# Loads of x in odd tiles dealt unevenly over the DMA engines, in a field-pair projection kernel

## Chip, core and metric

The kernel runs on one core of a Trainium2 chip. The metric is the device time of one execution in microseconds; for a program on one core that is the time of that core. The core has 16 DMA engines, numbered 0 to 15 in this text, and all its queues (SyncE's, ScalarE's, GpSimd's) send their work to these 16.

## What is computed

```python
# r_x: 2048 x 32 x 64 float32; W: 496 x 64 x 64 float32
PAIRS = list(combinations(range(32), 2))      # 496 pairs (i, j), i < j
xi = x[:, pi, :]                              # 2048 x 496 x 64
xj = x[:, pj, :]
proj = jnp.einsum('bpd,pod->bpo', xi, W)
return proj * xj                              # 2048 x 496 x 64
```

For each of 496 pairs of fields, field i is projected by the pair's 64x64 matrix and multiplied, element by element, by field j. The result has 2048 rows of 496 x 64 float32, 260 MB, and is by far the largest thing that moves; x is 16.8 MB and the weights 8.1 MB.

## The kernel before

The batch is cut into 16 tiles of 128 rows, and a row of the batch is a partition of SBUF. The weights are loaded once, in 13 pieces, into `w_sb`. A tile needs its x twice: as it is (`x_sb0` for even tiles, `x_sb1` for odd ones, 128 rows of 8 KB each), and turned (`x_t`), so that TensorE can multiply by it.

A tile is 21 steps (`plan`), each of which fills two halves of a PSUM buffer (`proj`, 2 buffers x 2 halves). TensorE (`project`) writes both halves. VectorE multiplies the first half by x and writes the product to a staging buffer (`staged`, L338). The second half goes the same way in every third step and in the last; in the other 14 (`pool_steps`) ScalarE copies it to the staging buffer (L258) and GpSimd multiplies it there by x (L232). Between step 9 and step 10 stands the item "turn": TensorE transposes the next tile's x (L270), and ScalarE copies the result to `x_t` (L247).

The steps are put together in 11 groups, and each group ends in one store of 128 rows (SyncE, L191), of 896 to 1952 KB; 11 stores a tile, 176 in all. The staging has 9 slots: groups 9 and 10 use the slots of groups 4 and 5. Before a slot is written again, `slot_free` waits until the store that reads it has landed on all engines (semaphore `stored`, 16 counts per store).

Each engine has its own instruction stream in program order, and each DMA issuer too. x is loaded as follows. The first tile's x comes in two halves from SyncE at the start (L195, L197). The second tile's x is the last DMA of SyncE's prologue (L205), 1 MB with 128 rows of 8 KB. From tile 1 on, GpSimd issues the load of the next tile's x (`load_x`, L219) ahead of its work of step 3 (`LOAD_BEFORE`), once VectorE and GpSimd have finished the tile before: 128 rows in one DMA, 14 times, for tiles 2 to 15. In an odd tile the next x goes to `x_sb0`, in an even one to `x_sb1`. TensorE waits for it ahead of the turn (L304, semaphores `x_loaded0` and `x_loaded1`). ScalarE issues one DMA in all, the identity for the transposes (L242).

The lines that the change touches are these; SyncE's last prologue load and GpSimd's load:

```python
sp.dma_start(x_sb[1][:], x[P:2 * P, :]).then_inc(x_second_loaded, 16)
...
pool.wait_ge(emptied[b][1], use + 1)
pool.wait_ge(pool_scaled[group_of[pool_steps[-1]]], tile.number)
pool.dma_start(x_sb[1 - tile.parity][:], x[bass.ds((tile.number + 1) * P, P), :]
              ).then_inc(x_loaded[1 - tile.parity], 16)
```

Of the kernel before, what the change touches and what calls it, by code (L numbers as in the profile page):

```python
# [9 lines left out]
P = 128  # L10
# [3 lines left out]
LOAD_BEFORE = 3  # L14
WARM_UP = 16

SHARED_SLOTS = {9: 4, 10: 5}


def pair_index(i, j, fields):  # L20
# [51 lines left out]
def field_pair_project(nc, x, w, ident, out, fields, dim):  # L72
    batch = x.shape[0]
    tiles = batch // P
# [11 lines left out]
    def items(tile):  # L86


        for n, item in enumerate(last_tile if tile.last else whole_tile):
            yield item, (1 + n) % 2, tile.number * per_tile + (1 + n) // 2  # L90


    pool_steps = [s for s in range(len(steps) - 1) if s % 3 != 2]
    group_of = {s: g for g, group in enumerate(groups) for s in group}

    def group_range(g):
        segments = [seg for s in groups[g] for unit in steps[s] for seg in unit]
        first = min(pair_index(i, j, fields) for i, j, _ in segments)
        assert sum(n for _, _, n in segments) == max(
            pair_index(i, j, fields) + n for i, j, n in segments) - first  # L100
        return first, sum(n for _, _, n in segments)

    slot_of = [SHARED_SLOTS.get(g, g) for g in range(len(groups))]
    slots = len(groups) - len(SHARED_SLOTS)
    assert sorted(set(slot_of)) == list(range(slots))
# [13 lines left out]
    def every_tile(emit):  # L119

        for t in range(tiles):
            emit(Tile(t, t % 2, t // 2, last=t == tiles - 1))

    def each_tile(eng, emit):

        emit(Tile(0, 0, 0))
        with eng.Fori(0, (tiles - 2) // 2) as t:
            emit(Tile(2 * t + 1, 1, t))
            emit(Tile(2 * t + 2, 0, t + 1))
        emit(Tile(tiles - 1, 1, tiles // 2 - 1, last=True))  # L130

    with ExitStack() as ctx:  # L132
        def sb(name, shape, dt=F32):
            return ctx.enter_context(nc.sbuf_tensor(name, shape, dt))

        def sem(name):
            return ctx.enter_context(nc.semaphore(name))
# [3 lines left out]
        x_sb = [sb(f"x_sb{h}", [P, fields * dim]) for h in range(2)]  # L141
# [7 lines left out]

        ident_loaded = sem("ident_loaded")  # L150
        x_first_loaded = [sem(f"x_first_loaded{h}") for h in range(2)]
        x_second_loaded = sem("x_second_loaded")

        x_loaded = [sem(f"x_loaded{h}") for h in range(2)]
        w_loaded = [sem(f"w_loaded{c}") for c in range(len(w_cuts) - 1)]
        filled = [[sem(f"filled{b}{h}") for h in range(2)] for b in range(2)]
        emptied = [[sem(f"emptied{b}{h}") for h in range(2)] for b in range(2)]

        pool_scaled = [sem(f"pool_scaled{g}") for g in range(len(groups))]
# [11 lines left out]
        def staged_part(s, i, j, n):  # L171
            g = group_of[s]
            to = (pair_index(i, j, fields) - group_range(g)[0]) * dim
            return staged[slot_of[g]][:, to:to + n * dim]

        @block.sync
        def _(sp):
            def emit(tile):
                where = {item: (b, use) for item, b, use in items(tile)}
                for g, group in enumerate(groups):  # L180
                    first, n = group_range(g)


                    pooled = any(s in pool_steps for s in group)
                    if pooled and g == 0:
                        sp.wait_ge(pool_scaled[g], tile.number + 1)
                    b, use = where[group[-1]]
                    sp.wait_ge(emptied[b][group[-1] not in pool_steps], use + 1)
                    if pooled and g > 0:
                        sp.wait_ge(pool_scaled[g], tile.number + 1)  # L190
                    sp.dma_start(out[bass.ds(tile.number * P, P), first * dim:(first + n) * dim],  # L191
                                 staged[slot_of[g]][:, 0:n * dim]).then_inc(stored[slot_of[g]], 16)

            half = fields * dim // 2
            sp.dma_start(x_sb[0][:, 0:half], x[0:P, 0:half]).then_inc(x_first_loaded[0], 16)  # L195
            sp.dma_start(w_sb[:, w_cuts[0]:w_cuts[1]], w[:, w_cuts[0]:w_cuts[1]]).then_inc(w_loaded[0], 16)
            sp.dma_start(x_sb[0][:, half:], x[0:P, half:]).then_inc(x_first_loaded[1], 16)  # L197
            for c in range(1, len(w_cuts) - 2):
                sp.dma_start(w_sb[:, w_cuts[c]:w_cuts[c + 1]], w[:, w_cuts[c]:w_cuts[c + 1]]
                             ).then_inc(w_loaded[c], 16)  # L200

            c = len(w_cuts) - 2
            sp.dma_start(w_sb[0:dim, w_cuts[c]:w_cuts[c + 1]], w[0:dim, w_cuts[c]:w_cuts[c + 1]]
                         ).then_inc(w_loaded[c], 16)
            sp.dma_start(x_sb[1][:], x[P:2 * P, :]).then_inc(x_second_loaded, 16)  # L205

            every_tile(emit)
            for k in range(slots):
                sp.wait_ge(stored[k], 16 * slot_uses[k] * tiles)

        @block.gpsimd
        def _(pool):
            def load_x(tile):

                _, b, use = list(items(Tile(tile.number - 1, 1 - tile.parity, None)))[-1]

                pool.wait_ge(emptied[b][1], use + 1)
                pool.wait_ge(pool_scaled[group_of[pool_steps[-1]]], tile.number)
                pool.dma_start(x_sb[1 - tile.parity][:], x[bass.ds((tile.number + 1) * P, P), :]  # L219
                              ).then_inc(x_loaded[1 - tile.parity], 16)  # L220

            def emit(tile):
                for item, b, use in items(tile):
                    if item == LOAD_BEFORE and not tile.first and not tile.last:
                        load_x(tile)
                    if item not in pool_steps:
                        continue
                    for i, j, n in steps[item][1]:
                        product = staged_part(item, i, j, n)

                        pool.wait_ge(emptied[b][1], use + 1)
                        last = nc.gpsimd.tensor_tensor(  # L232
                            product, product, x_sb[tile.parity][:, j * dim:(j + n) * dim], ALU.mult)
                    g = group_of[item]
                    if item == max(s for s in groups[g] if s in pool_steps):
                        last.then_inc(pool_scaled[g], 1)

            every_tile(emit)

        @block.scalar  # L240
        def _(act):
            act.dma_start(ident_sb[:], ident).then_inc(ident_loaded, 16)  # L242

            def turned_out(b, use, to):
                for h in range(2):
                    act.wait_ge(filled[b][h], use + 1)
                    nc.scalar.activation(x_t[to][:, h * (UNIT // P):(h + 1) * (UNIT // P), :].rearrange(  # L247
                        "p k b -> p (k b)"), proj[b][h][:], ACT.Copy).then_inc(emptied[b][h], 1)

            def emit(tile):  # L250
                for item, b, use in items(tile):
                    if item == "turn":
                        turned_out(b, use, 1 - tile.parity)
                    elif item in pool_steps:
                        (i, j, n), = steps[item][1]
                        slot_free(act, tile, group_of[item])
                        act.wait_ge(filled[b][1], use + 1)  # L257
                        nc.scalar.activation(staged_part(item, i, j, n), proj[b][1][:, 0:n * dim],  # L258
                                             ACT.Copy).then_inc(emptied[b][1], 1)

            turned_out(0, 0, 0)
            every_tile(emit)

        @block.tensor
        def _(pe):
# [31 lines left out]
            def emit(tile):  # L297
                for item, b, use in items(tile):
                    if item == "turn":

                        if tile.first:
                            pe.wait_ge(x_second_loaded, 16)
                        else:
                            pe.wait_ge(x_loaded[1 - tile.parity], 16 * (tile.half + tile.parity))  # L304
                        for h in range(2):
                            pe.wait_ge(emptied[b][h], use)
                            turn(b, 1 - tile.parity, h)
                    else:
                        project(tile, item, b, use)
# [64 lines left out]
```

## Time and profile before

| what | value |
|---|---|
| time, median of 3 runs | 690.63 us (690.4 to 691.05) |
| the profiled execution's own time | 690.38 us |
| its span, first to last instruction | 688.5 us |
| around the span | 1.9 us |
| TensorE busy | 591.9 us (86%) |
| VectorE, GpSimd, ScalarE busy | 412.2, 398.4, 207.4 us |
| DMA, mean over the span | 285.24 MB, 414 GB/s |
| stores and other traffic of SyncE's queue (q1) | 270.28 MB, 94.1% of 16 engines' span |
| GpSimd's queue (q0) | 14.68 MB, 5.1% |
| mean granted TensorE clock | 0.922 |

The share of DMA is the mean busy share of the 16 engines. A transfer's time is counted from its packet's start to its end, so that an engine that takes packets of two queues in turn counts a little twice; a share of 1.01 means that no engine stood idle. One engine of 16 alone is a share of 0.0625.

### The profile page before, as it was taken

What the parts mean: (1) busy time and instruction counts of PE and PEld (TensorE: products, weight loads), DVE (VectorE), ACT (ScalarE), POOL (GpSimd) and SP (SyncE); (2) the same over time, 40 slices, a digit from 0 to 9 for tenths busy, and PEclk for the clock granted to TensorE, in tenths of its full rate; (3) what the DMA queues carried; (4) which work ended last, traced back from release to release, by engine and by line L of the source; (5) the groups of instructions that cost most, each with busy time, mean ns of one, the idle gap of its engine ahead of it and who ended that gap; (6) DMA issues with size and microseconds to landing.
All of it is one profiled execution on the core that took longest, in us unless ns stands there. A gap on an engine that the chain in (4) does not pass through costs nothing.

```text
span 688.5 us, 7590 instructions
## 1 busy us (share of the span) xinstructions
PE 591.9 (86%) x2704; PEld 365.3 (53%) x2704; DVE 412.2 (60%) x528; ACT 207.4 (30%) x257; POOL 398.4 (58%) x242
## 2 busy tenths in 40 slices
PE   6969897988979799797997979899797997989962
PEld 4536464545555465465555545465464655555531
DVE  1646574774738657374684747657475683747751
ACT  2412333233222333233233232332332333232320
POOL 0745575574655846476574655846466574755841
PEclk9998999999989989898999999999898998989985
DMA  8999999999999999999999999999999999999995
GB/s 341 391 428 428 420 427 421 427 419 427 428 416 429 415 426 421 422 427 420 428 416 429 424 415 428 399 426 385 410 429 413 428 420 428 430 412 428 421 425 244
DMA packets 29765, 285.24 MB, mean 414 GB/s; under 512 B 3312, under 2 KB 3440, under 8 KB 7216
## 3 DMA queue, kind: packets, MB, share of 16 engines
q1 hardware_dynamic: 27584, 270.28, 94.1%
q0 software_dynamic: 2016, 14.68, 5.1%
q14 instruction: 16, 0.13, 0.0%
q8 instruction: 5, 0.08, 0.0%
q10 hardware_dynamic: 144, 0.07, 0.0%
HBM read 24.97 MB, written 260.05 MB: 414 GB/s over the span
## 4 chain that ended last, share of the span: by engine, by line
PE 46%; DMA 38%; POOL 7%; ACT 4%; DVE 3%; issue 1%; DVEq 0%; ACTq 0%; SPq 0%
PE proj L292 42%; DMA out_dram<-staged 26%; DMA x_sb<-x_dram 11%; POOL staged L232 7%; ACT staged L258 3%; PE proj L270 3%; DVE staged L338 3%; DMA ident_sb<-ident_dram 1%; PE proj L313 1%; ACT x_t L247 0%; ACTq L257 0%; DVEq L132 0%; DVEq L335 0%; SPq L190 0%
## 5 line engine op out<-in xcount | busy, mean ns | idle before, releaser
L338 DVE TENSOR_TENSOR staged<-proj,x_sb 128x1024 f32<-128x1024 f32 (+7 forms) x528 | 412.2, 828 | 265.5 <-PE proj L292 220.3
L292 PE MATMUL proj<-w_sb,x_t 64*128 64x512 f32 (+7 forms) x2432 | 537.4, 543 | 26.3 <-DVE staged L338 24.8
L232 POOL TENSOR_TENSOR staged<-staged,x_sb 128x1024 f32<-128x1024 f32 (+4 forms) x224 | 390.6, 1753 | 275.0 <-ACT staged L258 272.5
L292 PEld LDWEIGHTS proj<-w_sb,x_t 64*128 64x128 f32 x2432 | 315.7, 193 | 242.9 <-issue 134.5
L258 ACT ACTIVATE staged<-proj 128x1024 f32<-128x1024 f32 (+4 forms) x224 | 173.7, 787 | 382.3 <-PE proj L292 329.7
L270 PE MATMUL proj<-ident_sb,x_sb 128*128 128x128 f32 x256 | 52.1, 388 | 52.2 <-DMA x_sb<-x_dram 52.2
L270 PEld LDWEIGHTS proj<-ident_sb,x_sb 128*128 128x128 f32 x256 | 46.4, 205 | 61.4 <-DMA x_sb<-x_dram 61.4
L247 ACT ACTIVATE x_t<-proj 128x1024 f32<-128x1024 f32 x32 | 32.4, 1023 | 80.5 <-PE proj L270 80.5
L313 PE MATMUL proj<-ident_sb 128*128 128x128 f32 x16 | 3.7, 425 | 5.7 <-DMA ident_sb<-ident_dram 5.7
L219 POOL DMA_DIRECT2D x_sb<-x_dram x14 | 8.4, 601 | 0.0
L313 PEld LDWEIGHTS proj<-ident_sb 128*128 128x128 f32 x16 | 3.3, 228 | 5.6 <-DMA ident_sb<-ident_dram 5.6
L247 ACT ACT_TABLE_LOAD x1 | 1.3, 1283 | 1.2 <-PEq L368 1.2
L368 POOL MEMSET const-float32-0.0<- 128x1 f32 x1 | 0.1, 98 | 0.2 <-issue 0.2
L368 POOL MEMSET const-bfloat16-1.0<- 128x1 bf16 x1 | 0.1, 101 | 0.0
L368 POOL MEMSET const-uint8-127<- 128x1 uint8 x1 | 0.1, 101 | 0.0
L368 POOL MEMSET const-float32-1.0<- 128x1 f32 x1 | 0.1, 98 | 0.0
## 6 DMA issues: line engine op xcount, KB each, us to landing
out_dram<-staged SPq DMA_DIRECT2D x16, 1952.0 KB, 14.4
out_dram<-staged SPq DMA_DIRECT2D x16, 1824.0 KB, 16.4
out_dram<-staged SPq DMA_DIRECT2D x16, 1728.0 KB, 13.6
out_dram<-staged SPq DMA_DIRECT2D x16, 1696.0 KB, 17.0
out_dram<-staged SPq DMA_DIRECT2D x16, 1568.0 KB, 16.5
out_dram<-staged SPq DMA_DIRECT2D x16, 1440.0 KB, 17.8
out_dram<-staged SPq DMA_DIRECT2D x16, 1312.0 KB, 11.8
out_dram<-staged SPq DMA_DIRECT2D x16, 1216.0 KB, 12.4
```

The costliest lines, as they stand in the source:

```text
L219: pool.dma_start(x_sb[1 - tile.parity][:], x[bass.ds((tile.number + 1) * P, P), :]).then_inc(x_loaded[1 - tile.parity], 16)
L232: last = nc.gpsimd.tensor_tensor(product, product, x_sb[tile.parity][:, j * dim:(j + n) * dim], ALU.mult)
L247: nc.scalar.activation(x_t[to][:, h * (UNIT // P):(h + 1) * (UNIT // P), :].rearrange("p k b -> p (k b)"), proj[b][h][:], ACT.Copy).then_i ...
L258: nc.scalar.activation(staged_part(item, i, j, n), proj[b][1][:, 0:n * dim], ACT.Copy).then_inc(emptied[b][1], 1)
L270: last = nc.tensor.transpose(proj[b][h][:, n * P:(n + 1) * P], x_sb[of][:, k * P:(k + 1) * P], ident_sb[:])
L292: last = nc.tensor.matmul(proj[b][h][:, at:at + width], x_t[tile.parity][half, i // 2, :], w_sb[half, col:col + width], start=True, stop=True)
L313: nc.tensor.transpose(proj[1][0][:, 0:P], ident_sb[:], ident_sb[:])
L338: last = nc.vector.tensor_tensor(staged_part(item, i, j, n), proj[b][h][:, at:at + n * dim], x_sb[tile.parity][:, j * dim:(j + n) * dim], ...
L368: nc = bacc.Bacc("TRN2", target_bir_lowering=False, num_devices=1)
```

## The change

In odd tiles (1, 3, ... 13), the next x no longer comes in one DMA of 128 rows. GpSimd loads 120 rows, then 1 row; ScalarE loads the last 7 rows, ahead of its own work of step 3, after the same two waits as GpSimd's. In tile 13 the numbers are 105, 13 and 10. Even tiles load 128 rows in one DMA as before. The second tile's x in the prologue comes in three parts: 112 rows and 12 rows from SyncE, and 4 rows from GpSimd as its first DMA, ahead of all its work. Each of the parts has a wait of its own on TensorE ahead of the turn. By the names in the diff, GpSimd's 120 rows go to all engines but engine 3 (`LEFT_OUT`), and the one row behind them to engine 3.

```diff
+LEFT_OUT = 3
+IN_STEP = LEFT_OUT + 1
+X_ROWS = (120, 1, 7)
+X_LAST_ROWS = (105, 16 - LEFT_OUT, 7 + LEFT_OUT)
...
+    def x_rows(tile):
+
+        if not tile.parity:
+            return (P,), 0
+        of = X_LAST_ROWS if tile.number == tiles - 3 else X_ROWS
+        assert sum(of) == P
+        return of[:-1], of[-1]
...
-            sp.dma_start(x_sb[1][:], x[P:2 * P, :]).then_inc(x_second_loaded, 16)
+            for row, rows in ((0, P - 16), (P - 16, 16 - IN_STEP)):
+                sp.dma_start(x_sb[1][row:row + rows, :], x[P + row:P + row + rows, :]
+                             ).then_inc(x_second_loaded, 16)
...
-                pool.dma_start(x_sb[1 - tile.parity][:], x[bass.ds((tile.number + 1) * P, P), :]
-                              ).then_inc(x_loaded[1 - tile.parity], 16)
+                row = 0
+                for rows in x_rows(tile)[0]:
+                    pool.dma_start(x_sb[1 - tile.parity][row:row + rows, :],
+                                   x[bass.ds((tile.number + 1) * P + row, rows), :]
+                                   ).then_inc(x_loaded[1 - tile.parity], 16)
+                    row += rows
+
+            pool.dma_start(x_sb[1][P - IN_STEP:, :], x[2 * P - IN_STEP:2 * P, :]).then_inc(x_in_step, 16)
...
+            def load_x_rest(tile):
+
+                _, b, use = list(items(Tile(tile.number - 1, 1 - tile.parity, None)))[-1]
+
+                act.wait_ge(emptied[b][1], use + 1)
+                act.wait_ge(pool_scaled[group_of[pool_steps[-1]]], tile.number)
+                rows = x_rows(tile)[1]
+                act.dma_start(x_sb[1 - tile.parity][P - rows:, :],
+                              x[bass.ds((tile.number + 2) * P - rows, rows), :]).then_inc(x_rest_loaded, 16)
...
+                    if item == LOAD_BEFORE and not tile.first and not tile.last and x_rows(tile)[1]:
+                        load_x_rest(tile)
...
-                            pe.wait_ge(x_second_loaded, 16)
+                            pe.wait_ge(x_second_loaded, 32)
+                            pe.wait_ge(x_in_step, 16)
+                        elif tile.parity:
+                            pe.wait_ge(x_loaded[0], 32 * tile.half + 32)
+                            pe.wait_ge(x_rest_loaded, 16 * tile.half + 16)
                         else:
-                            pe.wait_ge(x_loaded[1 - tile.parity], 16 * (tile.half + tile.parity))
+                            pe.wait_ge(x_loaded[1], 16 * tile.half)
```

On GpSimd, tile 1, ahead of step 3. `TENSOR_TENSOR` is a product of L232 (before) or L259 (after), `x_sb<-x_dram` the load. Before:

```order
L232 TENSOR_TENSOR staged<-staged,x_sb 128x1024 [waits emptied11]
L232 TENSOR_TENSOR staged<-staged,x_sb 128x896 [waits emptied01]
L219 DMA x_sb<-x_dram 128x2048 [waits pool_scaled9,emptied01]
L232 TENSOR_TENSOR staged<-staged,x_sb 128x768 [waits emptied01]
L232 TENSOR_TENSOR staged<-staged,x_sb 128x1024 [waits emptied11] x2
```

On GpSimd, the same place, now:

```order
L259 TENSOR_TENSOR staged<-staged,x_sb 128x1024 [waits emptied11]
L259 TENSOR_TENSOR staged<-staged,x_sb 128x896 [waits emptied01]
L242 DMA x_sb<-x_dram 120x2048 [waits pool_scaled9,emptied01]
L242 DMA x_sb<-x_dram 1x16x128
L259 TENSOR_TENSOR staged<-staged,x_sb 128x768 [waits emptied01]
L259 TENSOR_TENSOR staged<-staged,x_sb 128x1024 [waits emptied11] x2
```

A second DMA stands behind the first, with no wait; it is one row, written in the instruction as 16 pieces of 128 elements (512 B). In tile 13 its place is taken by one of 13x2048, and the first one's by 105x2048.

On ScalarE, the same item of tile 1. `ACTIVATE staged<-proj` is the copy that GpSimd's products wait for. Before:

```order
L258 ACTIVATE staged<-proj 128x1024 [waits filled11,stored0]
L258 ACTIVATE staged<-proj 128x896 [waits filled01,stored0]
L258 ACTIVATE staged<-proj 128x768 [waits filled01,stored1]
L258 ACTIVATE staged<-proj 128x1024 [waits filled11,stored2]
```

On ScalarE, now:

```order
L297 ACTIVATE staged<-proj 128x1024 [waits filled11,stored0]
L297 ACTIVATE staged<-proj 128x896 [waits filled01,stored0]
L284 DMA x_sb<-x_dram 7x2048 [waits pool_scaled9,emptied01]
L297 ACTIVATE staged<-proj 128x768 [waits filled01,stored1]
L297 ACTIVATE staged<-proj 128x1024 [waits filled11,stored2]
```

A DMA that waits for GpSimd's and VectorE's last work of the tile before now stands between two copies, seven times in the program.

## Rows read from the trace of the kernel before

**Rows 1.** Busy time by stage; columns: each engine (instructions), TensorE's clock, DMA share, GB/s
```profile
core 0: us, PE busy (x) PEld busy (x) DVE busy (x) ACT busy (x) POOL busy (x), PEclk, DMA share, GB/s
...
200.00:430.00 230.00, 205.83 (x946) 126.78 (x945) 142.19 (x186) 72.23 (x90) 134.92 (x82) 0.93 1.01 423
...
480.00:670.00 190.00, 168.21 (x765) 102.84 (x761) 117.83 (x150) 58.06 (x73) 114.74 (x69) 0.92 1.01 422
```

**Rows 2.** The same view, the end of the program
```profile
680.00:681.00 1.00, 0.00 (x0) 0.00 (x0) 0.00 (x0) 0.00 (x0) 0.00 (x0) 0.50 0.85 350
681.00:682.00 1.00, 0.00 (x0) 0.00 (x0) 0.00 (x0) 0.00 (x0) 0.00 (x0) 0.50 0.13 56
682.00:683.00 1.00, 0.00 (x0) 0.00 (x0) 0.00 (x0) 0.00 (x0) 0.00 (x0) 0.50 0.06 27
...
686.00:687.00 1.00, 0.00 (x0) 0.00 (x0) 0.00 (x0) 0.00 (x0) 0.00 (x0) 0.50 0.07 29
687.00:688.00 1.00, 0.00 (x0) 0.00 (x0) 0.00 (x0) 0.00 (x0) 0.00 (x0) 0.50 0.02 7
```

**Rows 3.** The last store of the program: issue, and time to landing
```profile
L191 SPq DMA_DIRECT2D out_dram<-staged x1: 333/333/333, 677.7 to 677.7; - x1
...
DMA to landing us min/median/max: 10.2/10.2/10.2
```

**Rows 4.** DMA packets between 681 and 688.5 us
```profile
DMA packets 29, 0.20 MB, mean 26 GB/s; under 512 B 6, under 2 KB 6, under 8 KB 19
```

**Rows 5.** Busy time by stage again, the stretches with gaps in the DMA
```profile
433.00:435.00 2.00, 2.00 (x10) 1.04 (x7) 2.00 (x3) 0.72 (x1) 2.00 (x2) 1.00 0.93 389
474.00:476.00 2.00, 2.00 (x14) 1.15 (x11) 1.43 (x2) 0.59 (x1) 2.00 (x2) 1.00 0.97 410
476.00:478.00 2.00, 2.00 (x11) 1.15 (x8) 2.00 (x3) 0.81 (x1) 2.00 (x2) 1.00 0.45 189
478.00:480.00 2.00, 2.00 (x12) 1.27 (x11) 1.61 (x3) 0.48 (x1) 1.98 (x2) 1.00 0.96 379
```

**Rows 6.** The page's DMA queues: packets, MB, share of 16 engines' span
```profile
q14 instruction: 16, 0.13, 0.0%
q8 instruction: 5, 0.08, 0.0%
```

**Rows 7.** The chain that ended last, its end: start, duration, what
```profile
654.17 15.98 DMA out_dram<-staged
...
670.17 0.90 DVE staged L338
...
676.64 0.99 DVE staged L338 x3
```

**Rows 8.** DMA issues: GpSimd's loads of x (L219), then ScalarE's one DMA (L242)
```profile
L219 POOL DMA_DIRECT2D x_sb<-x_dram x14: 591/591/720, 65.4 to 600.1; - x14
...
DMA to landing us min/median/max: 11.8/13.3/13.6
```
```profile
L242 ACTq DMA_DIRECT2D ident_sb<-ident_dram x1: 406/406/406, 0.7 to 0.7; - x1
```

**Rows 9.** Who waited for whom over the span: total, times, longest
```profile
PE proj L270 <- DMA x_sb<-x_dram: 52.2, 15, 4.2
...
DVE staged L338 <- DMA out_dram<-staged: 41.3, 22, 7.1
```

**Rows 10.** Timeline, start of tile 13: ScalarE, GpSimd, VectorE
```profile
555.46 0.92 ACT L258 ACTIVATE staged<-proj 128x896 f32<-128x896 f32 x1 [1.12 <-PE proj L292]
558.47 0.81 ACT L258 ACTIVATE staged<-proj 128x768 f32<-128x768 f32 x1 [2.09 <-PE proj L292]
```
```profile
548.66 2.76 POOL L232 TENSOR_TENSOR staged<-staged,x_sb 128x640 f32<-128x640 f32 x2 [0.47 <-ACT staged L258]
...
559.37 1.82 POOL L232 TENSOR_TENSOR staged<-staged,x_sb 128x768 f32<-128x768 f32 x1
562.41 2.37 POOL L232 TENSOR_TENSOR staged<-staged,x_sb 128x1024 f32<-128x1024 f32 x1 [1.22 <-ACT staged L258]
```
```profile
551.13 4.61 DVE L338 TENSOR_TENSOR staged<-proj,x_sb 128x448 f32<-128x448 f32 x9 [1.61 <-DMA out_dram<-staged]
```

More of the change, by code:

```diff
@@ L152, in field_pair_project @@
         x_second_loaded = sem("x_second_loaded")
+        x_in_step = sem("x_in_step")
         x_loaded = [sem(f"x_loaded{h}") for h in range(2)]
+        x_rest_loaded = sem("x_rest_loaded")
         w_loaded = [sem(f"w_loaded{c}") for c in range(len(w_cuts) - 1)]
```

## The prediction

> **What bounds the kernel now.** First the busy times by stage [rows 1]. From 200 to 430 us and from 480 to 670 us the share of the 16 DMA engines is 1.01, at 423 and 422 GB/s, while no compute engine is full (TensorE, the fullest, 168.2 of 190 us). An engine's packets queue without a gap, so compute could be somewhat faster or slower and the time would not move: the sum of the DMA work sets it. TensorE's and VectorE's waits for DMA [rows 9] are the back-pressure of that, not a cause.
>
> Second, the end [rows 2], read second by second. Up to 681 us nearly all engines work (0.85). From 682 us to the end the share is 0.06 to 0.07, and one engine of 16 is 0.0625: one engine is still busy while 15 are done. The packets say the same: 29 in the last 7.5 us, at 26 GB/s [rows 4], which is 423/16. The last store is issued at 677.7 and lands 10.2 us later, at 687.9 [rows 3]. So one engine is late, and the program ends with it.
>
> How late? The shares from 680 us on are 0.85, 0.13, 0.06, five more of this size down to 0.02, together 1.32 engine-sets, or 21.1 engine-us. The late engine has 7.5 of these (to 687.4, and its completion comes at 687.9), which leaves 13.6 for 15 engines: on average they end at 680.9, the last of them at about 682 (the 0.13 of 681 to 682 is two engines). The late one ends 7.0 us behind their mean. Besides, the others ran dry twice before [rows 5]: at 433 to 435 us, 389 GB/s where 423 is full, is 0.16 us lost; at 474 to 480 us, 410, 189 and 379 make 0.06 + 1.11 + 0.21. Together 1.5 us for all 16, so 1.6 us for the 15. At such a point stores wait for slots, and a slot is free only when its store has landed on all engines. So the late engine's excess of work is 7.0 + 1.6 = **8.6 us** over the mean of the others.
>
> A part of it has a name: instruction fetches, 21 packets with 0.13 + 0.08 MB [rows 6], 7.9 us at 26.5 GB/s if one engine serves them all. That they sit on one engine is my reading; the trace does not number its engines.
>
> **The price of a row.** 8192 B at 423/16 = 26.4 GB/s is 0.31 us of one engine.
>
> **What moves.** With the dealing that the diff names, engine 3 has 2 rows of each odd tile's x in place of 8 (1 of GpSimd's, 1 of ScalarE's): 7 loads x 6 rows = 42 rows less. In the prologue, 112 rows give each engine 7, 12 rows give one more to engines 0 to 11, and 4 rows one more to 0 to 3, so engine 3 has 9 instead of 8. Net 41 rows, **12.7 us less** on engine 3. They go elsewhere: ScalarE's 7 rows put one more on engines 0, 1, 2, 4, 5 and 6, each time but with tile 13's own sums; with the prologue each of these six gets 7 rows more in all, **2.2 us**. Engines 7 to 9 get one row more, 10 and 11 none, 12 to 15 one less. The check: 6 x 7 + 3 - 4 - 41 = 0.
>
> That this is how rows are dealt no row of the trace before shows, since each DMA there has 128 rows (or 64). The Trainium skill ("DMA: Bandwidth & Descriptors", "Why a DMA increments its semaphore by 16 and not by 1") agrees for the large parts: the number of engines is the largest up to 16 that divides the rows, GpSimd's DMAs start where a round-robin cursor stands, ScalarE's and SyncE's at the lowest engine. By that, 4 rows bring the cursor to 4, and 120 rows take 15 engines from there, all but engine 3.
>
> **The sum.** If engine 3 is the late one, its 12.7 us relief is more than its excess of 8.6, so it ends before the others, and the bound is the fullest of the other 15. Their mean ends at 680.9, minus 1.6 for the dry stretches that the late engine caused, plus 2.2 for the six: 681.5. The last of the others ends some 1.1 us behind their mean (682.0 against 680.9); if it is one of the six, 682.6. I take 682.1, the middle. The last landing moves from 687.9 to 682.1, **5.8 us** less; the span goes to 682.7, the execution to 684.6 (690.38 - 5.8), and against the median of 690.63, 0.25 above the profiled run, it is 684.8. Bounds: 1.6 not won back gives 686.4; with engine ends levelled better (680.9 - 1.6 + 0.9, where 0.9 is the 42 rows shared by 15 engines) 683.0.
>
> **What is added, and its cover.** GpSimd gets a second DMA issue, 0.59 us [rows 8], in 7 tiles. Behind it stands the product of step 3; the next product then waited 1.22 us for ScalarE [rows 10], so the delay ends there. ScalarE gets a DMA issue (0.41 us, rows 8's other row) behind two waits. In tile 13 its copy ends at 556.4, GpSimd's last product of the tile before at 551.4 and VectorE's at 555.7, so both waits are over, and 2.09 us of idle time for TensorE follow [rows 10]: nothing queued behind it is late. The copies and GpSimd's products behind it are who would wait otherwise. If the cover were gone, these cost up to 7 x 1.0 = 7 us of compute, which a DMA share of 1.01 hides as long as the stores' queue holds work. SyncE's one more prologue issue (0.6 us) and GpSimd's 4 rows fall into the start, where SyncE issues nothing for 10 us afterwards; 4 rows ahead of the first loads cost at most 0.31 us on an engine. Completions of the small DMAs are 4-byte packets and I cost them at nothing; twice as many for 7 loads could cost 0.2 us. x itself lands 11.8 to 13.6 us after its issue [rows 8], in turn with stores; engines 0 to 6 have 9 rows instead of 8, 0.3 us later at most, and TensorE's wait of 3.5 us per tile for it [rows 9] may grow by that without a DMA engine going idle.
>
> **What is late next.** The last stretch of compute now starts when a store of 654.17 lands, 15.98 us later, and takes 7.5 us from 670.17 to the last store [rows 7]. That landing is the late engine's too, so it moves forward with it, to some 664 us; 7.5 us later is 671.5, some 10 us before the engines have worked off their stores. The end stays with DMA work.
>
> **Rivals.**
>
> *A: engine 3 is not the late one, and the late one is among 0, 1, 2, 4, 5, 6.* Then it gets 7 rows more, 2.2 us, and the end moves from 687.9 to 690.1: 692.8 us, slower. For it: the trace names no engine, 6 of 16 are such. It decides from the first tile on; the sign needs only two rows' worth. Chance 0.11.
>
> *B: the late engine is one of 7 to 15.* It has 1 row more to 1 less, 0.3 us at most: 690.6, no difference, since the six loaded ones have 7 us of slack. The Trainium skill ("DMA: Bandwidth & Descriptors", "Latency and other measured facts") says that engines 7 and 15 are usually slower where GpSimd issues DMAs; by that rule this rival is the case. The trace shows one late engine, not two. Chance 0.12.
>
> *C: the one row does not go to one engine.* Its instruction carries 16 pieces of 512 B. If they are spread over all 16, engine 3 is skipped only in the first odd load, and each later load skips another engine. Engine 3 then has 8 + 1 rows in six of seven loads, so with the prologue 41 rows less become 0 (-7 + 6 + 1). If it is late, the time is 690.6, and up to 2.2 us more when the skipping begins elsewhere and never meets it: 690.6 to 692.8. By the Trainium skill's rule on the number of engines (same section as above), a slowest dimension of 16 takes 16 engines, which is this rival; against it stands that 105, 13 and 10 in tile 13 only bring the cursor back to 0 if the single rows moved it by one. Chance 0.15, half of it slower.
>
> **How the numbers follow.** The forecast has 0.62, 683.0 to 686.6, all faster. A measurement of this kernel can tell about 0.2% (1.4 us) from no change. Faster 0.62; same: B and half of C, 0.19; slower: A and half of C, 0.19. The predicted time is 684.8. The range reaches over the unchanged cases (to 691.3) to hold 0.81: 682.9 to 691.3.
>
> **What would show it.** Right: in the last 8 us the share falls from 0.9 to 0 within 2 us, with no stretch at 0.06; no gap like that at 476 us; the store whose slot the last stretch waits for lands in about 10 us, not 15.98; the last store of all lands within 4 to 6 us rather than 10.2. Wrong: the stretch at 0.06 is still there, as long (B, C) or longer (A). If it is gone and the time is still above 687, the cause is a full engine among the six, or holes in the DMA share in the stages of [rows 1].

## The result: slower by 0.8%

| | before | after |
|---|---|---|
| median | 690.62 us (690.4 to 691.05) | 696.52 us (695.75 to 696.97) |
| ratio | | 1.0083, interval 1.0066 to 1.0101 |
| profiled execution, span | 690.38, 688.5 us | 696.8, 695.0 us |
| granted TensorE clock, mean | 0.922 | 0.934 |

The forecast was 684.8 us, in a range of 682.9 to 691.3. The time came out 5.9 us above before, and 5.2 us above the range. The clock is no cause: it is a little higher than before.

### The profile page after: what moved, and what is told of

It reads as the page before. It is cut to its first block, busy times and chain, and to the rows that moved or that the text cites. A ratio compares the mean times of both kernels' runs of the same rounds, so it can differ in the third digit from the quotient of the medians.

```text
span 695.0 us, 7627 instructions
## 1 busy us (share of the span) xinstructions
PE 589.2 (85%) x2704; PEld 365.8 (53%) x2704; DVE 412.7 (59%) x528; ACT 207.6 (30%) x257; POOL 402.9 (58%) x250
## 4 chain that ended last, share of the span: by engine, by line
PE 45%; DMA 39%; POOL 7%; ACT 3%; DVE 3%; issue 1%; DVEq 0%; ACTq 0%; SPq 0%
PE proj L331 42%; DMA out_dram<-staged 28%; DMA x_sb<-x_dram 9%; POOL staged L259 6%; ACT staged L297 3%; PE proj L309 3%; DVE staged L381 3%; DMA ident_sb<-ident_dram 1%; PE proj L356 1%; POOL x_sb L242 0%; ACT x_t L274 0%; ACTq L296 0%; DVEq L148 0%; SPq L209 0%; DVEq L378 0%
## 5 line engine op out<-in xcount | busy, mean ns | idle before, releaser
L259 POOL TENSOR_TENSOR staged<-staged,x_sb 128x1024 f32<-128x1024 f32 (+4 forms) x224 | 391.0, 1756 | 276.2 <-ACT staged L297 273.9
L309 PE MATMUL proj<-ident_sb,x_sb 128*128 128x128 f32 x256 | 49.8, 376 | 60.6 <-DMA x_sb<-x_dram 60.6
L309 PEld LDWEIGHTS proj<-ident_sb,x_sb 128*128 128x128 f32 x256 | 44.7, 199 | 69.6 <-issue 36.2
L242 POOL DMA_DIRECT2D x_sb<-x_dram x21 | 11.8, 567 | 0.0
L247 POOL DMA_DIRECT2D x_sb<-x_dram x1 | 0.7, 698 | 0.8 <-POOLq L411 0.8
```

Source lines behind the costliest of these rows:

```text
L242: pool.dma_start(x_sb[1 - tile.parity][row:row + rows, :], x[bass.ds((tile.number + 1) * P + row, rows), :]).then_inc(x_loaded[1 - tile.pa ...
L247: pool.dma_start(x_sb[1][P - IN_STEP:, :], x[2 * P - IN_STEP:2 * P, :]).then_inc(x_in_step, 16)
L259: last = nc.gpsimd.tensor_tensor(product, product, x_sb[tile.parity][:, j * dim:(j + n) * dim], ALU.mult)
L309: last = nc.tensor.transpose(proj[b][h][:, n * P:(n + 1) * P], x_sb[of][:, k * P:(k + 1) * P], ident_sb[:])
```

## The profile after

Busy time by stage, of the changed kernel (columns: the stretch in us, its length, busy time and instructions of each engine, TensorE's clock, DMA share, GB/s). The first stretch is in the prologue, the others answer to [rows 1] and [rows 2]:

```profile
24.00:33.00 9.00, 6.01 (x30) 3.29 (x28) 5.09 (x7) 2.43 (x3) 7.79 (x4) 1.00 1.02 306
...
480.00:670.00 190.00, 168.74 (x783) 104.59 (x780) 122.22 (x154) 59.06 (x74) 119.38 (x73) 0.96 1.00 415
...
686.00:687.00 1.00, 0.00 (x0) 0.00 (x0) 0.00 (x0) 0.00 (x0) 0.00 (x0) 0.50 1.01 422
687.00:688.00 1.00, 0.00 (x0) 0.00 (x0) 0.00 (x0) 0.00 (x0) 0.00 (x0) 0.50 0.58 243
688.00:689.00 1.00, 0.00 (x0) 0.00 (x0) 0.00 (x0) 0.00 (x0) 0.00 (x0) 0.50 0.18 74
689.00:690.00 1.00, 0.00 (x0) 0.00 (x0) 0.00 (x0) 0.00 (x0) 0.00 (x0) 0.50 0.07 29
...
693.00:694.00 1.00, 0.00 (x0) 0.00 (x0) 0.00 (x0) 0.00 (x0) 0.00 (x0) 0.50 0.05 22
```

The stretch at 0.06 is still there, from 689 us to the end: one engine is still late, and the whole end of the program lies some 6 us further back. The stage rate from 480 to 670 us fell from 422 to 415 GB/s, at a share of 1.00 instead of 1.01. (It does not tell the cause: prologue_only, below, has the same 415 there, and is 4 us faster.) The others still run dry, at another place (the same view of after), 172 GB/s where 423 is full:

```profile
398.00:400.00 2.00, 2.00 (x9) 1.14 (x9) 1.92 (x3) 0.58 (x1) 1.99 (x4) 1.00 0.43 172
```

The last store of the program, after, answering to [rows 3]; issued 6.4 us later, and again 10.2 us to its landing:

```profile
L210 SPq DMA_DIRECT2D out_dram<-staged x1: 332/332/332, 684.1 to 684.1; - x1
...
DMA to landing us min/median/max: 10.2/10.2/10.2
```

The compute side held. ScalarE's timeline after, start of tile 13, answering to [rows 10]; the new DMA is issued in 0.29 us while the first of the two copies shown still runs (to 563.44 us), and the next copy waits 2.09 us for TensorE, to the hundredth what it waited before:

```profile
562.52 0.92 ACT L297 ACTIVATE staged<-proj 128x896 f32<-128x896 f32 x1 [0.48 <-PE proj L331]
562.60 0.29 ACTq L284 DMA_DIRECT2D x_sb<-x_dram  x1
565.53 0.81 ACT L297 ACTIVATE staged<-proj 128x768 f32<-128x768 f32 x1 [2.09 <-PE proj L331]
```

So the loss is DMA work again, as in the kernel before, and two questions stand. Which engine is late, and how many rows does it get? And what costs the rest, since even the 7 more rows of rival A are 2.2 us and not 5.9?

## Which engine is late

The trace does not number its engines. A small DMA of k rows from SyncE, behind the last store, can: if its rows lie on the k lowest engines, its semaphore is complete only when each of these has worked off its stores. The Trainium skill ("DMA: Bandwidth & Descriptors", "Why a DMA increments its semaphore by 16 and not by 1") says that SyncE's and ScalarE's DMAs use the lowest-numbered k engines, where k is the largest number up to 16 that divides the rows. For k = 1 the probe has 17 rows, which by this all lie on engine 0.

### probe_before

```diff
@@ SyncE, behind the last store
+for k in range(1, 17):
+    rows = 17 if k == 1 else k
+    sp.dma_start(x_sb[0][0:rows, (k - 1) * 64:k * 64], ident[0:rows, 0:64]).then_inc(probed[k - 1], 16)
@@ GpSimd, at its end
+for k in range(1, 17):
+    pool.wait_ge(probed[k - 1], 16)
+    nc.gpsimd.memset(x_sb[0][:, 1100 + k:1101 + k], 0.0)
```

> The kernel before, with 16 tiny loads behind the last store on SyncE's queue: the k-th has k rows (the first 17 rows, a prime) of 256 B, meant to run on the k lowest-numbered DMA engines, each with a semaphore of its own; GpSimd, which has nothing left to do, waits for them in turn and writes one column after each. A load that includes the late engine lands with it, some 6 us after those without. If the late engine is number e, the first e columns are written within about 2 us of each load's issue (680 to 683 us), and column e+1 only at about 688. Theory (engine 3 is late): columns 1 to 3 early, 4 late. Rival A (0, 1, 2, 4, 5 or 6): the jump at another of the first seven. Rival B: the jump at 8 to 16. Time: 690.6 to 692.

Measured 694.16 us (one run, 2 us above the expected 692; the 16 probes themselves take time). GpSimd's timeline at the end (start, busy time, what, and in brackets the idle time ahead of the group and its releaser):

```profile
682.35 0.45 POOL L245 MEMSET x_sb<- 128x1 f32 x3 [8.26 <-DMA x_sb<-ident_dram]
683.32 0.10 POOL L245 MEMSET x_sb<- 128x1 f32 x1 [0.52 <-DMA x_sb<-ident_dram]
688.73 2.18 POOL L245 MEMSET x_sb<- 128x1 f32 x12 [5.31 <-DMA x_sb<-ident_dram]
```

The memsets stand in the order of k. Four come at 682 to 683 us, and the fifth is held up for 5.31 us, with all behind it: **the late engine is number 4**. Engines 0 to 3 are among the early ones; of 5 to 15 the probes say nothing more, since each of the later ones also waits for engine 4. The number rests on the skill's rule of the lowest engines; the first_engine and rows_0to3 runs below fit it.

### probe_after

> The changed kernel with the same 16 tiny loads at its end. The late engine is the same as in the kernel before, and its lag behind the others at the end is 5 to 6 us again: the jump stands at the same column. If the lateness is no property of one engine but of where the work falls, it stands elsewhere. Time: 696.5 to 698.

The same probes on the changed kernel: 701.03 us (one run), and the same order in GpSimd's timeline, so the late engine is again number 4:

```profile
690.76 0.10 POOL L272 MEMSET x_sb<- 128x1 f32 x1 [0.46 <-DMA x_sb<-ident_dram]
694.92 2.18 POOL L272 MEMSET x_sb<- 128x1 f32 x12 [4.06 <-DMA x_sb<-ident_dram]
```

## Where GpSimd's rows go

### onerow3, onerow4, after_left4 and onerow4_late

Is it enough to leave out the right engine, and to keep the single row in one piece? `onerow3` is the changed kernel with that row as 2047 elements (an odd number, which 16 equal pieces can't share; its trace shows 7 packets of 8188 B, one a load), its last element loaded by ScalarE, and 120, 1 and 7 rows in all odd tiles:

```diff
-        of = X_LAST_ROWS if tile.number == tiles - 3 else X_ROWS
+        of = X_ROWS
...
+                    wide = fields * dim - (rows == 1)
+                    pool.dma_start(x_sb[1 - tile.parity][row:row + rows, 0:wide],
+                                   x[bass.ds((tile.number + 1) * P + row, rows), 0:wide]
```

> The changed kernel, but GpSimd's single row is 2047 elements in one piece (a prime's multiple that does not split into 16), so that it takes one engine and moves the cursor by one; ScalarE loads the last element; all seven odd loads are 120, 1 and 7 rows, and 12 rows of 256 B at the end bring the cursor back. If engine 3 is late and only the spread row broke the dealing (rival C), engine 3 is relieved by 12.7 us and the time is 685 to 688 (the forecast, plus 1 to 2 us of the new prologue). If engine 3 is not the late one, the dealing holds but the late engine gets the same extra rows as before: 693 to 697.

696.27 us (695.78 to 697.33), ratio 1.0084 (1.0071 to 1.0098): as the changed kernel. `onerow4` has `LEFT_OUT = 4` besides, and `after_left4` is the changed kernel with that one number changed.

> As onerow3 (the single row stays on one engine), but with engine 4 left out in place of 3; the prologue is 112 rows, 11 rows and GpSimd's 5. The probes put the late engine fifth from the lowest, number 4. If that is the late one and GpSimd's cursor counts as the other queues do, it is relieved by 12.7 us and the end is set by the others: 681.5 plus 2 for the prologue, 685.5 to 688. If GpSimd counts otherwise, or the lateness does not depend on the rows given, 693 to 697 as onerow3 (696.3).

> The changed kernel with LEFT_OUT = 4 and nothing else: the single row is still 16 pieces. If these are spread over all engines and the cursor drifts (rival C), engine 4 is skipped once only, and the time is 694 to 697, near the changed kernel's 696.5. If the single row does go to one engine, it is as onerow4.

697.18 us (696.68 to 697.45), 1.0091 (1.0077 to 1.0104), and 697.28 us (696.93 to 697.62), 1.0093 (1.0077 to 1.0108). Leaving out the engine that the probes name does not relieve it. Both are even some 0.8 us slower than with 3: GpSimd's DMA in the prologue has 5 rows there, and by the dealing found below the fifth lies on engine 4, 0.31 us; the rest of the 0.8 is open. `onerow4_late` keeps the prologue of before and brings the supposed cursor to its place by a DMA of 5 short rows in tile 0:

```diff
+pool.dma_start(step_sb[0:IN_STEP, :], ident[0:IN_STEP, 0:64]).then_inc(x_in_step, 16)
```

> As onerow4, but with the prologue of the kernel before (the second x in one DMA), and the cursor moved by a DMA of 5 rows of 256 B that GpSimd issues in tile 0 ahead of step 3, once the loads of the start are through. If the first DMA of GpSimd and the three-part second x cost 1.9 us, as prologue_only measured, this is 1.5 to 2.5 us faster than onerow4: 683.5 to 686. If the prologue's cost was hidden, the same as onerow4.

694.95 us (694.27 to 695.37), 1.0057 (1.0044 to 1.0071). Some 2 us of onerow4's loss sat in the prologue; the rest stayed. So not only the number of the engine was wrong, but the dealing itself.

### one_engine and one_engine3

Before, with probes; in the 7 odd tiles GpSimd also loads 17 rows of 3584 B and 15 rows of 256 B. By the prediction's rule all 17 rows (a prime number) go to one engine, where the cursor stands, and the probes would show it late.

```diff
+pool.dma_start(junk_sb[:], x[0:17, 0:896]).then_inc(junked[0], 16)
+pool.dma_start(step_sb[0:15, :], ident[0:15, 0:64]).then_inc(junked[1], 16)
```

> The kernel before with the 16 probes at its end, and in each of the 7 odd tiles two more DMAs from GpSimd behind the load of x: 17 rows of 3584 B and 15 rows of 256 B, to memory that nothing reads. If 17 rows (a prime) go to one engine, from GpSimd's cursor, and 15 bring the cursor back, one and the same engine gets 61 KB more seven times, 2.3 us each, 16 us in all, more than the late engine's 8.6: the probes show a second late engine, and which it is tells where the cursor stood. If the cursor starts at 0, already column 1 is late. If GpSimd deals 17 rows as 2 to each of 9 engines, no engine becomes late by it, and the jump stays at column 5 alone; 17 rows then never show 272 packets of 4 B beside them.

697.31 us (one run). GpSimd's queue in its trace holds, beside the usual loads, 56 packets of 7168 B, 7 of 3588 B and 49 of 8 B. I read these as, for each of the seven loads of 17 rows, 8 packets of 2 rows, 1 of 1 row (with 4 B of completion), and 7 dummy packets, with which the engines without a row fill in: engines take ceil(17/16) = 2 rows each until there are none left, nine of them in all. No single engine got all 17. `one_engine3` moves a cursor by 3 rows first and by 13 at the end:

> As one_engine, but GpSimd's first DMA has 3 rows, and one of 13 at the end brings the cursor back. If the cursor works as supposed, the second late engine is 3 further (mod 16) than in one_engine. If the dealing does not depend on a cursor, the probes show the same as in one_engine.

698.11 us, and again the fifth probe is the first that is held up. This says little about the cursor, since nine engines share the 17 rows and none of them becomes the latest wherever they begin; the next run decides.

### first_engine

Does each of GpSimd's DMAs begin at the same engine? Before, with probes, and behind each load of x seven DMAs of one row of 887 elements (98 rows of 3548 B):

```diff
+pool.wait_ge(junked, 7 * 16 * (tile.number - 1))
+for n in range(7):
+    pool.dma_start(junk_sb[n:n + 1, :], x[n:n + 1, 0:887]).then_inc(junked, 16)
```

> The kernel before with the 16 probes at its end, and behind each of GpSimd's 14 loads of x seven DMAs of one row of 3548 B (887 elements, a prime, so one piece), to memory that nothing reads: 98 such rows, 0.13 us each, 13 us. Theory now: GpSimd deals every direct copy from engine 0, ceil(rows/16) rows to each, and has no cursor. Then all 98 are on engine 0, it is late by more than the old one, and already the first probe lands late, with all others. Rival (a cursor that moves by one with each): 98 rows are spread as 6 to each engine, none becomes late by it, and the jump stays at the fifth.

710.31 us (one run), and GpSimd's timeline at the end is one group:

```profile
696.29 2.77 POOL L251 MEMSET x_sb<- 128x1 f32 x16 [14.81 <-DMA x_sb<-ident_dram]
```

All 16 probes are held up, so an engine that all of them use is now the last, and that is engine 0 alone. The 98 rows are 13 us of work for one engine, and 0.8 us each if a cursor spread them. So they went to **engine 0**: each of these DMAs starts there, wherever the last one ended. (The time rose by 19.5 us, more than rows on engine 0 explain; where the rest went was not looked into.)

If GpSimd's larger DMAs start there too, 120 rows are 8 on each of engines 0 to 14 and none on 15. The trace of after fits: GpSimd's queue has 8 more 4-byte packets for each load of 120 rows (beside the 16 of its completion), 8 dummies for one engine, and 96 packets of 512 B, the single row of six tiles in 16 pieces each. Which engine has the dummies the trace does not say. Engine 4 keeps its 8 rows of each odd load, and ScalarE's 7 rows, on engines 0 to 6, add one. With the sixteenths of the single row and tile 13's own numbers that is 7.4 rows, 2.3 us, more than before. The same section of the Trainium skill, which the prediction used for the cursor, has the rule of ceil(rows/16) rows per engine as an exception; the packets here agree with the exception, and the cursor did not show in any run.

### rows_0to3

If so, the loss by rows must go when ScalarE's and GpSimd's small loads stay on engines 0 to 3. The changed kernel with 120, 4 and 4 rows in all odd tiles:

```diff
-X_ROWS = (120, 1, 7)
-X_LAST_ROWS = (105, 16 - LEFT_OUT, 7 + LEFT_OUT)
+X_ROWS = (120, 4, 4)
+X_LAST_ROWS = (120, 4, 4)
```

> The changed kernel with 120, 4 and 4 rows in all odd loads, in place of 120, 1 and 7 (105, 13 and 10). If GpSimd and ScalarE both deal from engine 0, the two parts of 4 rows lie on engines 0 to 3, and engine 4, the late one, has 8 rows as before the change, 7 rows (2.2 us) less than in the changed kernel: 694 to 695. If the dealing follows a cursor, or the rows on the late engine are not what costs, 696 to 697.

694.14 us (693.9 to 694.47), ratio 1.005 (1.0036 to 1.0063): 2.4 us less than after, where 2.3 are the rows. This edit also takes away the row in 16 pieces and tile 13's own numbers, but onerow3 had neither and took 696.27 us, as the changed kernel. So it is **shown** that the rows which ScalarE's part puts on engine 4 cost some 2.3 of the 5.9 us.

## What costs the other 3.6 us

### prologue_only and prologue_sp

Before, with the prologue of after alone (112 and 12 rows from SyncE, 4 from GpSimd):

```diff
-sp.dma_start(x_sb[1][:], x[P:2 * P, :]).then_inc(x_second_loaded, 16)
+for row, rows in ((0, P - 16), (P - 16, 12)):
+    sp.dma_start(x_sb[1][row:row + rows, :], x[P + row:P + row + rows, :]).then_inc(x_second_loaded, 16)
...
+pool.dma_start(x_sb[1][P - 4:, :], x[2 * P - 4:2 * P, :]).then_inc(x_in_step, 16)
```

> The kernel before with the new prologue alone: the second tile's x as 112 and 12 rows from SyncE and 4 from GpSimd as its first DMA. In the changed kernel's trace every prologue load lands 1 us later and the second x 2.2 us later than before. If that start is what costs, this kernel alone is 1 to 2.5 us slower: 691.6 to 693.1. If it is absorbed (the late engine's own work sets the end and only one row is added to it), at most 0.4 us: 690.6 to 691.0.

692.58 us (692.17 to 693.16), ratio 1.0027 (1.0018 to 1.0036), **1.9 us more**. And with 112 and 16 rows from SyncE, nothing from GpSimd:

> The kernel before with the second tile's x as 112 and 16 rows, both from SyncE, and nothing from GpSimd: of prologue_only's +1.9 us, this leaves the second DMA and takes away GpSimd's first one. If the cost is GpSimd's DMA among the first loads, 690.7 to 691.2; if it is the split of the second x, 692 to 693.

691.95 us (691.48 to 692.57), 1.0018 (1.0008 to 1.0027), 1.1 us more. All engines get the same number of rows there, so it is not a matter of how many. The stretch 24 to 33 us, in which the second x is loaded, first before, then prologue_sp (busy time by stage, columns as above):

```profile
24.00:33.00 9.00, 8.45 (x45) 5.19 (x44) 5.31 (x7) 4.06 (x5) 8.02 (x4) 1.00 1.01 353
```
```profile
24.00:33.00 9.00, 6.68 (x32) 3.86 (x29) 5.54 (x7) 2.58 (x4) 7.99 (x4) 0.94 1.01 294
```

The share is 1.01 in both, but the same busy engines move 294 instead of 353 GB/s: 59/423 of 9 us is 1.3 us, about the measured 1.1. The second x's packets of 8192 B took 561 ns on average, 437 before (552 in after, which has 306 GB/s there): 128 packets times 124 ns over 16 engines are 1.0 us. This holds in every trace taken: 531 to 578 ns in the eight with the second x in parts, 415 to 450 in the eleven with it in one DMA. Cutting this load makes its packets slower, and no engine is idle. The 0.8 us between the two experiments I put down to GpSimd's DMA among the first loads. The 736 KB piece of the weights lands 13.0 us after its issue in prologue_only and 11.9 in prologue_sp (11.8 before, 13.0 after). The two also differ by 4 of SyncE's rows, and their times overlap (from 692.17, and up to 692.57), so the size is rough.

### split_only and split_pool

Before, with the odd loads dealt evenly but in two parts: 112 rows from GpSimd, 16 from ScalarE.

```diff
+rows = P - 16 * tile.parity
+pool.dma_start(x_sb[1 - tile.parity][0:rows, :], x[bass.ds((tile.number + 1) * P, rows), :]
...
+act.dma_start(x_sb[1 - tile.parity][P - 16:, :], x[bass.ds((tile.number + 2) * P - 16, 16), :]
```

> The kernel before, with the odd tiles' x as 112 rows from GpSimd and 16 from ScalarE: 7 and 1 row on each engine, 8 as before, so that only the split itself is added, a second DMA behind two waits on ScalarE. If the split costs nothing on the late engine, 690.4 to 691.1. If it is what made the changed kernel slower by more than its rows and prologue (some 2 us), 692 to 693.

692.7 us (691.96 to 693.26), ratio 1.0027 (1.0015 to 1.0038): **1.8 us more**, with 8 rows per engine as before. The same cut, but both parts from GpSimd:

> The kernel before with the odd tiles' x as 112 and 16 rows, both from GpSimd (split_only had the 16 rows from ScalarE and took 692.7). If the cost of a split is that of one more DMA whatever its queue, 692 to 693. If it is that of a third queue that the engines take in turn, or of ScalarE's waits, 690.5 to 691.2.

691.31 us (690.84 to 691.62), 1.0009 (1.0000 to 1.0018): 0.5 us, at the edge of what can be told from no difference. So most of it comes with ScalarE as the issuer: 0.26 us a load with it (1.8 by 7), 0.07 without. Slower packets of x are not the reason here: they take 310 ns on either queue, as in one DMA before (GpSimd's mean is 310 to 311 in all three traces). The same 112 and 16 rows are thus slowed in the prologue and not here. What the trace of split_only shows instead is DMA engines that run dry more often; one stretch, then the stage from 480 us on, where before has 1.01 and 422:

```profile
520.00:522.00 2.00, 2.00 (x8) 1.08 (x8) 1.92 (x3) 0.81 (x1) 1.98 (x3) 1.00 0.32 127
```
```profile
480.00:670.00 190.00, 169.55 (x770) 103.33 (x766) 118.69 (x151) 58.36 (x73) 115.11 (x69) 0.92 1.00 418
```

Counted from 60 us until most engines have ended, 3.6 us of all engines' time is idle, 2.0 before and 0.9 in split_pool (one execution each). Why a part on ScalarE's queue does this and one on GpSimd's does not **stays open**.

### x_by_sp

One explanation of that would be the queues taking turns on the engines. Before, with all loads of x issued by SyncE ahead of the tile's first store, on the same queue as the stores:

```diff
+if g == 0 and not tile.first and not tile.last:
+    ...
+    sp.dma_start(x_sb[1 - tile.parity][:], x[bass.ds((tile.number + 1) * P, P), :]
```

> The kernel before with all loads of x issued by SyncE, on the stores' queue, ahead of the tile's first store: no rows of two queues are taken in turn any more, and no row moves to another engine. If taking turns between a load and a store is what costs (the trace of before has 345 to 385 GB/s in two windows of 2 us behind an x load, where 425 is usual, some 0.3 us per load and more), it is 2 to 6 us faster: 685 to 689. If the loss lies in reading x itself, or the queue adds a wait for x that empties the engines, 690 to 693.

690.97 us (690.56 to 691.82), 1.0003 (0.9994 to 1.0012): no difference. A second queue beside the stores costs nothing that this shows; a third one, or small parts in it, remains possible.

## Another way to relieve engine 4

By the rule on SyncE's DMAs above, 68 rows are 17 on each of engines 0 to 3, and 60 rows 4 on each of 0 to 14. A store of 128 rows cut so gives engine 4 four rows instead of 8, and engines 0 to 3 have 21. Applied to one late store, this would level the end, if the number of rows were all that counts.

### tail_g6 and tail_g10

```diff
+cuts = [0, 68, P] if tile.last and g == 6 else [0, P]
+for lo, hi in zip(cuts, cuts[1:]):
+    sp.dma_start(out[bass.ds(tile.number * P + lo, hi - lo), ...], staged[slot_of[g]][lo:hi, 0:n * dim])
```

> The kernel before with one store of the last tile (group 6, rows of 9.25 KB) dealt as 68 and 60 rows from SyncE. By the probes SyncE deals from engine 0; 68 = 4 x 17 rows then lie on engines 0 to 3 (17 each) and 60 on 0 to 14 (4 each), so the late engine 4 has 4 rows instead of 8, 1.4 us less, and engines 0 to 3 have 21, 4.7 us more, within the 6 us that they end earlier. Theory: the end moves forward by 1.4 us less a DMA's cost of 0.1 to 0.3: 689.3 to 689.8. If the late engine is not as the probes say, or a store on few engines holds its slot too long, 690.8 or more.

695.77 us (694.33 to 696.61), ratio 1.0061 (1.0047 to 1.0075): 4 to 5 us slower. The theory fell; only the "690.8 or more" of the other case holds, and it named no such size. Group 6's packets, 9472 B, took 526 ns on average instead of 360, the longest 1364 ns. One stretch of it, then the same of before:

```profile
665.00:670.00 5.00, 0.00 (x0) 0.00 (x0) 0.00 (x0) 0.00 (x0) 0.00 (x0) 0.73 1.03 369
```
```profile
665.00:670.00 5.00, 0.00 (x0) 0.00 (x0) 0.00 (x0) 0.00 (x0) 0.00 (x0) 0.61 1.01 422
```

Again a full share and fewer bytes. With the last store cut so (`g == 10`):

> As tail_g6 with the very last store (group 10, rows of 7 KB): the late engine has 1.1 us less, engines 0 to 3 have 3.5 us more. 689.7 to 690.1, and nothing waits for its slot but the end. If engines 0 to 3 then end last, or the split costs as much as it brings, 690.6 to 691.2.

691.45 us (689.8 to 692.71), 1.0006 (0.9997 to 1.0015), no difference. Its eleven times spread over 2.9 us, those of before over 1.0. In its profile, which is of the fastest of them (689.8; the end of the program, by stage), the stretch at 0.06 is gone, and instead four or five engines end late, as engines 0 to 3 with 21 rows would (0.28 is 4.5 engines of 16):

```profile
685.00:686.00 1.00, 0.00 (x0) 0.00 (x0) 0.00 (x0) 0.00 (x0) 0.00 (x0) 0.50 0.28 110
686.00:687.00 1.00, 0.00 (x0) 0.00 (x0) 0.00 (x0) 0.00 (x0) 0.00 (x0) 0.50 0.10 43
```

The dealing can thus be moved. The last store's packets of 7168 B took 332 ns instead of 274 even in this fastest run; that slower packets are what eats the gain in the others is argued, since none of these was profiled. Nothing that was run is faster than the kernel before.

## The sum, as it stands

| part | us | from |
|---|---|---|
| second x in parts | 1.1 | prologue_sp |
| GpSimd's DMA among the first loads | 0.8 | prologue_only less prologue_sp |
| odd loads in parts, one from ScalarE | 1.8 | split_only |
| 7.4 rows more on engine 4 (by count) | 2.3 | after less rows_0to3 measured 2.4 |
| sum | 6.0 | measured 5.9 |

`onerow4_late`, which has the last two (1.8 and 7 rows, 2.2), should be at 694.9 and is at 694.95.

The third part is borrowed from a kernel with other parts (112 and 16 rows), and that it is the same loss in the changed kernel is not shown. There GpSimd's packets of x are slower in the odd loads (319 ns, 310 in the even ones), and the stores' packets beside them too (42.7 ns per KB, 41.5 before), which split_only does not have. What is measured is that rows_0to3, with the new prologue and the odd loads in parts but no more rows on engine 4, is 3.3 us above before, of which prologue_only has 1.9. That the four parts meet the total within 0.1 us is in part luck.

## Why the prediction was wrong, point by point

**What bounds the kernel.** Right: the DMA engines, with one that is late at the end, and compute has room. The probes confirm the one late engine, and the added issue on ScalarE delayed nothing at the start of tile 13. The 8.6 us of excess are 0.5 too many: 7.0 sets a landing (687.9) against the others' last packets, and the late engine's own last packet ends at 687.4; nothing hung on it. The fetches of instructions as a part of engine 4's excess remain a reading.

**The price of a row.** Right: 0.31 us by the rate, and GpSimd's packets of 8192 B take 310 ns on average; 7.4 rows came to 2.4 us.

**The step that failed.** "With the dealing that the diff names, engine 3 has 2 rows of each odd tile's x in place of 8." By the dealing that the runs point to, engine 3 has 9, as have all from 0 to 6; the one that is left out is 15, and the rows start at 0 each time. The 12.7 us of relief never were. The second half, "If engine 3 is the late one", was wrong as well: it is 4. Either alone is enough to take the whole gain away.

**What is added, and its cover.** ScalarE's issue was indeed covered, where it was looked at. The terms "4 rows ahead of the first loads cost at most 0.31 us" and "Completions of the small DMAs ... I cost them at nothing; twice as many for 7 loads could cost 0.2 us" were mis-sized: the prologue costs 1.9 us, and a part on ScalarE's queue 1.8 in split_only. The sum took a row as costing the same whatever DMA it comes in. The runs show that cutting the second x slows its packets (561 ns for 437), and that 16 rows apart on ScalarE's queue cost time without that. TensorE's waits for x ahead of the turn grew from 52.2 to 60.6 us over the 15 turns, about twice the 0.3 us a tile that was foreseen; that they cost time is not shown.

**What is late next.** The last store still lands 10.2 us after its issue; nothing moved forward.

**The rivals.** A had the right mechanism (the late engine is among 0, 1, 2, 4, 5, 6 and gets 7 rows, 2.2 us) and gave 692.8; the other 3.7 us are the two terms above. B was wrong in the number of the engine; neither 7 nor 15 is the late one. C was right in that the row is spread (96 packets of 512 B), but not in what follows, since there is no cursor that could drift. The range ended at 691.3 because A's 0.11 was left out, and no case had a loss by splitting.

**What would show it.** "Wrong: the stretch at 0.06 is still there, as long (B, C) or longer (A)": it is there, and the test points the right way.

## What to carry to other kernels

Before rows are moved between DMA engines, find by a ladder of small probing DMAs which engine is late, and by packet sizes in the trace how a queue deals its rows; both can be read in one run each, and a plan that rests on either unseen has nothing under it. Of the forms tried here, one DMA of 128 rows was the cheapest: cutting it cost 0.5 to 1.8 us even where every engine's sum of rows stayed the same. Where the DMA share is full, look at GB/s beside it, because slower packets show only there.

## What was not expected of the hardware

- GpSimd's plain copies give ceil(rows/16) rows to an engine: 17 rows lie on nine engines, and the other seven get dummy packets. Its DMAs of one row all start at engine 0 (98 of them held up all 16 probes); that those of 4, 17 and 120 rows start there as well fits rows_0to3 and is not shown by itself.
- SyncE's load of 128 rows cut in 112 and 16 moved 294 GB/s instead of 353 at a full share (packets of 8192 B: 561 instead of 437 ns). The same cut in GpSimd's loads left them at 310 ns. A store cut in 68 and 60 rows had packets of 526 instead of 360 ns. That engines then meet at the same part of the SBUF is one explanation. The Trainium skill ("DMA: Bandwidth & Descriptors", "The descriptor swizzle") says that in a transfer to 128 partitions each engine writes one port of the SBUF. No run here shows the ports, and GpSimd's 310 ns speak against this as the whole cause; it stays argued.
- Sixteen rows of a load cost 0.26 us when they go apart on ScalarE's queue, 0.07 us on GpSimd's. The cause is open.
- One DMA of 4 rows from GpSimd among the first loads cost some 0.8 us (prologue_only less prologue_sp).
